# Hand-overs inside a four-stage kernel: products, rows, slots and weights put in another place

## The chip, the cores and the metric

One core of a Trainium2 chip. The metric is the device time of one execution in microseconds. Lower is better.

## The reference

Four stages, each with a layer norm, a shift and scale by condition rows, and a gated residual sum. The numbers are float32.

- stage 1 (`B, T, E = 4, 1024, 256`): a state-space layer with 512 inner channels and 16 states; its output `y * silu(z) @ W_out` is added to `x`
- stage 2: 8 experts, top 2 of each token
- stage 3: causal attention, 8 heads of 128, over 1024 tokens of each of the 4 batches
- stage 4: 16 experts with a capacity of 640 rows each, top 2 of each token, ranks counted in token order

```python
q = q + pe[None, None]
k = k + pe[None, None]
scores = jnp.where(causal, q @ k.T / sqrt(D), -inf)
out = (softmax(scores) @ v) @ Wo.T
...
ranks = cumsum(onehot)[sel] - 1
slot = jnp.where(ranks < capacity, flat_sel * capacity + ranks, sentinel)
padded = zeros.at[slot].set(x_rep)
h = gelu(einsum(padded, w1)); out_padded = einsum(h, w2)
```

## The kernel before

One program with one instruction stream for each engine; semaphores order them. The phases follow each other: state space (to about 976 us), routing and experts of layer 0 (to 1378), attention of layer 1 with the routing of layer 1 inside it (to 2585), experts of layer 1. Between phases all engines meet.

**State space, its end.** A chunk is 512 tokens, there are 8. For each of 64 steps (`STEPS`) ScalarE makes a decay in a PSUM bank (`da_ps`, a ring of four), VectorE scans it and multiplies by C (`output`, writing `hc`), and TensorE sums it into `y_ps` (`sum_states`). Then `y` is copied, turned back (`turn_back`), copied again, gated on POOL in two halves (`gate_y`, blocks 0 and 1, then 2 and 3), and `out_product` multiplies it by `w_out`, four blocks and one product with the identity that adds `x`, for each of the chunk's four 128-token tiles. For chunks 0 to 6 this lies inside the next chunk's steps; for the last one nothing runs beside it. `hc_at` and `w_ready` count what it waits for.

**Attention.** The unit is the query tile, 128 queries of one head: `N = 64` of them in a batch (`HEADS` 8 by `TPB` 8), tile `n` with `n % 8` giving how many of the key tiles it sees. The four batches are unrolled for the first and last, and a loop for the two between (`batches`). For tile `n` TensorE emits, in this order: `score(n)`; a piece of the projection of the next head (`project`, six pieces a head: two of q, two of k, two of v, at `n % 8` in `PROJECT`); `turn(n - 2)`, which transposes the normalised probabilities; `turn_rows` of the next batch's layer-norm rows at `TURN`; `weigh`, the product with the values, six tiles behind. VectorE masks and takes the maximum (`maximum(n)`), normalises tile `n - 1`, takes the projected pieces to SBUF (`take_piece`), keeps the outputs (`keep`). ScalarE does the exponentials and copies what TensorE has turned. Scores go through two PSUM tensors of two banks, `s_ps`; the pieces of head 0 (`bank`) and the output products of a batch's end go through the same ones, the pieces of heads 1 to 7 through `qk_ps`.

At a batch's end `output(t)` makes 8 products (16 instructions) for each of eight 128-token tiles; two of them (`EARLY_OUT`) come ahead of the last weighing. VectorE gates and adds each (`out_added`). The next batch's pieces of head 0 wait for all of these, and `score(0)` for all six pieces.

At the start of the phase VectorE adds two halves of the sum of layer 0 (`sums0`, `more0`), tile by tile, takes statistics of eight tiles, normalises eight rows, TensorE turns each through one bank, ScalarE copies it to `h_b`, and then all six pieces of head 0 are projected. The sync engine's queue loads, in this order: the four halves of `x` and `more`, the condition rows of three kinds for four batches (`load_mods`), the gate weights, the positions, `w_o`, then the next batch.

**Routing inside attention.** The routing of batch `b - 1` is laid out over the query tiles of batch `b`: rows at `R_NORM`, logits at `R_PAIR`, picks at `PICK`, the count of ranks on TensorE at `RANK = 52`, and on VectorE at `SLOTS` the weights (tile 52), the ranks (53) and the slots (54). POOL then sends, for each of the eight 128-token tiles of the batch, two indirect transfers (`scatter`, one for each choice) to `slots1`, both after the score of one query tile. The rows of batch `b + 1` are normalised on VectorE from tile `NORM = 53` on.

**Last experts.** 16 experts in turn; two sets of weights (`w1`, `w2`) and of rows (`xs`) are held. At the start of the phase the queue loads the gates' rows, then for experts 0 and 1 the routed rows and both weights.

## Time and profile before

| | us |
|---|---|
| median of three runs | 2908.6 |
| lowest, highest | 2907.63, 2910.3 |
| the profiled execution's own time | 2909.66 |
| its span, first to last instruction | 2907.9 |
| TensorE busy, of the span | 2492.8 (86%) |
| VectorE busy | 2103.6 (72%) |
| ScalarE busy | 1296.4 (45%) |
| POOL busy | 1234.4 (42%) |
| mean granted clock of TensorE, of full speed | 0.932 |

PE is TensorE's matmul part, PEld its weight loads, which overlap it, DVE is VectorE, ACT ScalarE, POOL GpSimd, SP the sync engine; SPq is its queue of transfers. A float32 product counts as two PE instructions, a transpose as one. An idle time in brackets stands before the instruction whose row it is in, with what ended it. A granted clock of 1.00 is 2.4 GHz, 0.50 is 1.2 GHz.

### The profile page before, as it was taken

The page shows a single profiled execution, that of the slowest core. Times are in us where ns is not written, and L with a number is a line of the kernel's source. Part 1 is how long each engine was busy: PE and PEld are TensorE (multiplying, and loading weights), DVE is VectorE, ACT ScalarE, POOL GpSimd, SP SyncE. Part 2 cuts the span into 40 slices and gives each one's busy share as a digit, 9 for nine tenths or more (in the row PEclk, how much of TensorE's full clock was granted, in tenths as well). Part 3 has the DMA queues.
Part 4 walks back from the last instruction along what each step waited for, and adds up shares of the span by engine and source line. Part 5 has one row for each costly group of instructions (what it writes and reads, how often), then busy time and mean ns, then how long its engine had stood idle before and what let it go on. Part 6 is the DMA issues. An engine that isn't in the chain of part 4 may idle for free. (4 is left out here: it accounts for less than half of the span.)

```text
span 2907.9 us, 39192 instructions
## 1 busy us (share of the span) xinstructions
PE 2492.8 (86%) x12341; PEld 1792.0 (62%) x12342; DVE 2103.6 (72%) x4277; ACT 1296.4 (45%) x2563; POOL 1234.4 (42%) x531
## 2 busy tenths in 40 slices
PE   6677867868766759998799999999999999959998
PEld 4355545645545559998466666666666666647776
DVE  4999999999999566665666567766776677655554
ACT  4677677677665235554243324332433243311111
POOL 2799999999999036666000000020002000223344
PEclk8889989889986879999899999999999999969999
DMA  4645555555556254334300010001001000035554
GB/s 147 192 154 186 178 174 186 176 171 192 165 180 206 81 173 64 64 63 61 114 1 1 1 48 1 1 31 34 1 1 34 15 1 1 30 112 128 129 130 74
DMA packets 150845, 268.98 MB, mean 92 GB/s; under 512 B 18316, under 2 KB 107324, under 8 KB 150172
## 3 DMA queue, kind: packets, MB, share of 16 engines
q1 hardware_dynamic: 121916, 227.12, 24.3%
q0 software_dynamic: 28224, 37.78, 7.7%
q10 hardware_dynamic: 544, 2.10, 0.2%
q8 instruction: 81, 1.33, 0.2%
q14 instruction: 80, 0.66, 0.1%
HBM read 209.52 MB, written 57.43 MB: 92 GB/s over the span
## 5 line engine op out<-in xcount | busy, mean ns | idle before, releaser
L765 POOL TENSOR_TENSOR dbx<-u,b_all 128x2048 f32<-128x2048 f32 x128 | 578.6, 4535 | 71.2 <-DVE u L844 33.3
L1805 POOL DMA_INDIRECT slots<-at_r_rows,slot_of x64 | 62.7, 980 | 1140.3 <-DVE slot_of L2220 1048.5
L649 ACT ACTIVATE da_ps<-delta,a_neg 128x512 f32<-128x512 f32 x512 | 347.9, 689 | 132.7 <-DVE hc L917 124.5
L2066 ACT COPY at_pt<-at_pt_ps 128x512 f32<-128x512 f32 (+3 forms) x384 | 171.7, 483 | 504.5 <-PE at_pt_ps L1935 501.1
L469 PE MATMUL y_ps<-ident,hc 128*128 128x128 f32 x1536 | 246.5, 305 | 87.6 <-DVE hc L917 87.0
L1924 PE MATMUL at_s_ps<-at_qk 128*128 128x512 f32 (+3 forms) x768 | 291.4, 489 | 3.1 <-DVE at_v L2269 3.1
L1948 PE MATMUL at_o_ps<-at_pt,at_v 128*128 128x512 f32 (+3 forms) x768 | 288.6, 487 | 0.3 <-issue 0.3
L469 PEld LDWEIGHTS y_ps<-ident,hc 128*128 128x128 f32 x1536 | 200.6, 158 | 143.0 <-DVE hc L917 115.4
L2055 ACT ACTIVATE at_probs<-at_s_ps,at_small 128x128 f32<-128x128 f32 (+7 forms) x256 | 192.2, 751 | 202.2 <-DVE at_small L2280 198.9
L917 DVE TENSOR_TENSOR hc<-da_ps,c_all 128x512 f32<-128x512 f32 x384 | 257.7, 673 | 0.0
L907 DVE TENSOR_TENSOR_SCAN da_ps<-da_ps,state,dbx 128x512 f32<-128x512 f32 x192 | 243.4, 1277 | 4.5 <-ACT da_ps L649 3.6
L907 DVE TENSOR_TENSOR_SCAN da_ps<-da_ps,dbx 128x512 f32<-128x512 f32 x192 | 231.9, 1217 | 12.8 <-ACT da_ps L649 8.0
L1924 PEld LDWEIGHTS at_s_ps<-at_qk 128*128 128x128 f32 x768 | 137.0, 190 | 127.0 <-issue 94.9
L1908 PE MATMUL at_qk_ps<-at_h_b,w_qkv 128*128 128x512 f32 x448 | 211.9, 595 | 1.5 <-DVE at_rank L2206 0.9
L2276 DVE TENSOR_TENSOR at_s_ps<-at_s_ps,at_later 128x128 f32<-128x128 f32 x256 | 75.9, 296 | 187.0 <-PE at_s_ps L1924 186.0
L1534 POOL DMA_INDIRECT out<-e_ys,e_row_i x80 | 125.3, 1566 | 193.2 <-DVE e_ys L1643 153.6
L2278 DVE TENSOR_REDUCE at_small<-at_s_ps 128x1 f32<-128x128 f32 (+7 forms) x256 | 194.0, 758 | 8.8
L1935 PEld LDWEIGHTS at_pt_ps<-ident,at_probs 128*128 128x128 f32 x1152 | 137.1, 141 | 73.0 <-issue 52.0
L1935 PE MATMUL at_pt_ps<-ident,at_probs 128*128 128x128 f32 x1152 | 169.5, 274 | 9.5 <-DVE at_probs L2288 9.1
L1591 ACT ACTIVATE e_hid<-e_h_ps 128x320 f32<-128x320 f32 x128 | 55.9, 437 | 249.0 <-PE e_h_ps L1557 248.5
L1948 PEld LDWEIGHTS at_o_ps<-at_pt,at_v 128*128 128x128 f32 x768 | 127.4, 191 | 60.6 <-issue 57.2
L774 POOL TENSOR_TENSOR own_h<-own_h,c_all 128x2048 f32<-128x2048 f32 x32 | 144.9, 4528 | 29.5 <-DVE own_h L907 29.5
(385 smaller groups left out, 5021.6 us busy)
## 6 DMA issues: line engine op xcount, KB each, us to landing
b_all<-bc_rows SPq DMA_DIRECT2D x128, 512.0 KB, 4.4
c_all<-bc_rows SPq DMA_DIRECT2D x128, 512.0 KB, 5.1
e_w<-L_ffn_w SPq DMA_DIRECT2D x32, 512.0 KB, 5.5
slots<-zeros SPq DMA_DIRECT2D x40, 260.0 KB, 6.1
e_xs<-slots SPq DMA_DIRECT2D x16, 650.0 KB, 7.1
w<-L_ffn_W SPq DMA_DIRECT2D x24, 384.0 KB, 8.6
more<-zeros SPq DMA_DIRECT2D x16, 256.0 KB, 5.4
sums<-x SPq DMA_DIRECT2D x8, 512.0 KB, 6.9
```

Source lines behind the costliest of these rows:

```text
L469: mm = nc.tensor.matmul(y_ps[par][:, at], source[:, at], sh.ident[:], start=False, stop=(last and j == CT - 1), is_transpose=True)
L649: nc.scalar.activation(da_ps[s % RING_DA][:], delta[:, c % 2, m, :], ACT.Exp, scale=sh.a_neg[:, m, n:n + 1]).then_inc(S["da_ready"], 1)
L765: nc.gpsimd.tensor_tensor(dbx[:, at % RING_DBX], pair, rows, ALU.mult).then_inc(S["dbx_ready"], 1)
L907: nc.vector.tensor_tensor_scan(out, h, dbx[:, at % RING_DBX, i // 2, par, :], 0.0 if c % CPB == 0 else state[:, s:s + 1], ALU.mult, ALU.ad ...
L917: nc.vector.tensor_tensor(hc[:, v % RING_H, :], da_ps[s % RING_DA][:], c_all[:, at % RING_C, s % GS // 2, :], ALU.mult).then_inc(S["hc_rea ...
L1908: last = nc.tensor.matmul(out, w_qkv[:, k, h, i // 2, :], h_b[:, i % 2, k, :], start=(k == 0), stop=(k == KE - 1))
L1924: last = nc.tensor.matmul(s_ps[n % 2][:, part * CH:end], qk[:, h % 2, 0, i * P:(i + 1) * P], qk[:, h % 2, 1, part * CH:end], start=True, s ...
L1935: last = nc.tensor.transpose(pt_ps[half][:, j % CT, :], probs[:, n % 3, j * P:(j + 1) * P], sh.ident[:])
L1948: last = nc.tensor.matmul(o_ps[:, first:], v[:, h % 2, j, :], pt[half][:, j, first:], start=(j == 0), stop=(j == (half + 1) * CT - 1))
L2055: nc.scalar.activation(probs[:, n % 3, 0:(i + 1) * P], s_ps[n % 2][:, 0:(i + 1) * P], ACT.Exp, bias=small[:, n % 4, 1:2], scale=SCALE, acc ...
L2066: nc.scalar.copy(pt[i // CT][:, half * CT:half * CT + m, at], pt_ps[half][:, 0:m, :]).then_inc(S[f"copied{half}"], 1)
L2278: nc.vector.reduce_max(small[:, n % 4, 0:1], s_ps[n % 2][:, 0:(i + 1) * P], AX_X).then_inc(S["max_taken"], 1)
```

## The change

It has six parts. (1) The output products of the last chunk of the state-space phase go to the banks `da_ps`, and the identity and blocks 0 and 1 of each tile are multiplied ahead of the last gate, two tiles of them between the last steps. (2) At the start of attention the first batch goes in two halves: its condition rows are loaded first, the first half is added in one instruction on VectorE, the second in one on POOL; three pieces of head 0 are projected from the first four rows; the pieces' order is 0, 2, 4, 1, 3, 5; other loads wait for the second half. (3) The pieces of head 0 of later batches wait for their own bank alone, and `score(0)` for five pieces. (4) At tiles 64 and 65 the first seven heads' part of two output tiles is multiplied, ahead of the turns. (5) The slots are made at two tiles, weights earlier, the next batch's rows two tiles later; in batches 1 and 2 a scatter is sent after each of sixteen query tiles, in the last batch two after each of eight. (6) `w1`, `w2` and the gates' rows of the last experts lie in the place of `w_qkv` and are loaded after its last use; the first routed rows are loaded alone.

```diff
+            def last_first_blocks(j):
+                pair, i = j // 2, j % 2
+                if i == 0:
+                    pe.wait_ge(S["hc_ready"], hc_at(LAST, STEPS - RING_DA + pair) + 1)
+                    pe.wait_ge(S["y_gated"], LAST * HALVES + 1)
+                    pe.wait_ge(S["w_ready"], B)
+                out = da_ps[pair][:, i * E:(i + 1) * E]
+                nc.tensor.matmul(out, sh.ident[:], sh.x[:, LAST * CT + j, :], start=(i == 0), stop=False, skip_group_check=True)
+                for k in range(2):
+                    nc.tensor.matmul(out, u[:, LAST % 2, k, j * P:(j + 1) * P], sh.w_out[:, k, :], start=False, stop=False, skip_group_check=True)
+
+            def last_blocks(pair):
+                if pair == 0:
+                    pe.wait_ge(S["y_gated"], CHUNKS * HALVES)
+                for i in range(2):
+                    j = pair * 2 + i
+                    for k in range(2, MD):
+                        mm = nc.tensor.matmul(da_ps[pair][:, i * E:(i + 1) * E], u[:, LAST % 2, k, j * P:(j + 1) * P], sh.w_out[:, k, :],
+                                              start=False, stop=(k == MD - 1), skip_group_check=True)
+                mm.then_inc(S["out_done"], 1)
...
                     sum_states(c, k)
+                    if c == LAST and k >= STEPS - 3 and k < STEPS - 1:
+                        last_first_blocks(k - STEPS + 3)
...
-                turn_back(CHUNKS - 1, m)
+                turn_back(LAST, m)
+            for j in range(2, CT):
+                last_first_blocks(j)
             for pair in range(2):
-                out_product(CHUNKS - 1, pair)
+                last_blocks(pair)
...
+                bank = da_ps[pair] if c == CHUNKS - 1 else proj_ps[pair]
...
-                if not early(e, 2):
-                    sp.wait_ge(y_done, (e - 1) * S1)
+                if early(e, 2):
+                    return
+                sp.wait_ge(y_done, (e - 1) * S1)
...
             load(0, 0, 0)
+            sp.wait_ge(x_in[0], 16)
             load(1, 1, 0)
...
-        SLOTS = (RANK, RANK + 1, RANK + 2)
-        NORM, TURN, COPY = N - 11, N - 8, N - 7
+        SLOTS = (RANK - 2, RANK + 1, RANK + 2, RANK + 3)
+        NORM, TURN, COPY = N - 9, N - 8, N - 7
...
+            sp.dma_start(sh.mods[:, 0:2, 0, :], d["mod_rows"][1, 0:2, 0].partition_broadcast(P)).then_inc(S["mods0_in"], 16)
             for th in range(CPB):
...
-            load_mods(sp, d, sh, 1, 0, S["mods_in"])
+            sp.wait_ge(x_first[1], 32)
+            sp.dma_start(pos[:], d["posT"]).then_inc(S["pos_in"], 16)
+            sp.dma_start(sh.mods[:, 0:2, 1:B, :], d["mod_rows"][1, 0:2, 1:B].partition_broadcast(P)).then_inc(S["mods_in"], 16)
+            sp.dma_start(sh.mods[:, 2], d["mod_rows"][1, 2].partition_broadcast(P)).then_inc(S["mods_in"], 16)
             sp.dma_start(gate_w[:], d["gate_wT"].rearrange("(k p) n -> p k n", p=P)).then_inc(S["gate_in"], 16)
-            sp.dma_start(pos[:], d["posT"]).then_inc(S["pos_in"], 16)
             sp.dma_start(w_o[:], d["woT"].rearrange("(h p) e -> p h e", p=P)).then_inc(S["w_o_in"], 16)
...
+            sp.wait_ge(S["qk_done"], B * HEADS * PIECES + 1)
+            sp.dma_start(sh.gates[:], d["mod_rows"][1, 5].partition_broadcast(P)).then_inc(sh.gates_in, 16)
+            for e in range(2):
+                sp.dma_start(sh.w1[:, e], d["L1_ffn_w1"][e].rearrange("(k p) f -> p k f", p=P)).then_inc(sh.w1_in[e], 16)
+                sp.dma_start(sh.w2[:, e], d["L1_ffn_w2"][e].rearrange("(m p) f -> p m f", p=P)).then_inc(sh.w2_in[e], 16)
             store_out(B - 1)
...
+            late = slice(CT, TPB)
+            pool.wait_ge(x_first[1], 32)
+            nc.gpsimd.tensor_tensor(sh.x[:, late], sh.x[:, late], more[:, late], ALU.add).then_inc(first_summed[1], 1)
...
-                    if count is None:
-                        pool.wait_ge(S["scored"], (rb + 1) * N + SLOTS[2] + 1 + j)
                     for k in range(2):
+                        if count is None:
+                            pool.wait_ge(S["scored"], (rb + 1) * N + SLOTS[3] + 1 + (2 * j + k if rb < B - 2 else j))
                         nc.gpsimd.indirect_dma_start(out=d["slots1"], out_offset=bass.IndirectOffsetOnAxis(ap=sh.slot_of[:, k, i:i + 1], axis=0),
                                                      in_=r_rows[:, j, :], in_offset=None).then_inc(S["scattered"], 16)
...
+        FIRST_PIECES = (0, 2, 4, 1, 3, 5)
+        first_turned = (qk_ps, o_ps)
...
+            return qk_ps[:] if h else bank(FIRST_PIECES.index(i))
...
-            pe.wait_ge(S["w_o_in"], 16)
...
+                    out = first_turned[j % 2]
+                    pe.wait_ge(S["h_copied"], max(j, 1))
...
+            for j in range(CT):
                 turn_rows(0, j)
...
-                    if h > 0:
+                    if h > 1 or i > 0:
                         pe.wait_ge(S["qk_ready"], b * (HEADS * PIECES) + h * PIECES + i + 1)
-                    elif i >= 4:
-                        pe.wait_ge(S["qk_ready"], b * (HEADS * PIECES) + i - 2)
+                    else:
+                        pe.wait_ge(S["qk_ready"], b * (HEADS * PIECES) + h * PIECES + i)
+                    products(h, i, out)
...
+                def project_first(place):
+                    if place >= 4:
+                        pe.wait_ge(S["qk_ready"], b * (HEADS * PIECES) + place - 2)
+                    elif not first_batch:
+                        pe.wait_ge(S["out_added"], b * TPB + place - 2)
+                    products(0, FIRST_PIECES[place], bank(place))
...
-                        pe.wait_ge(S["qk_ready"], b * (HEADS * PIECES) + h * PIECES + (4 if h else PIECES) + 1)
+                        pe.wait_ge(S["qk_ready"], b * (HEADS * PIECES) + h * PIECES + (4 if h else PIECES - 1) + 1)
+                    if n == CT:
+                        pe.wait_ge(S["qk_ready"], b * (HEADS * PIECES) + PIECES + 1)
...
+                    if HEADS - 1 in heads:
+                        last.then_inc(S["out_done"], 1)
+
+                if first_batch:
+                    pe.wait_ge(S["h_copied"], CT + 1)
+                    for place in range(PIECES // 2):
+                        project_first(place)
+                    for j in range(CT, TPB):
...
+                for place in range(PIECES // 2 if first_batch else 0, PIECES):
+                    project_first(place)
...
+                    if n >= N:
+                        if n == N:
+                            if first_batch:
+                                pe.wait_ge(S["w_o_in"], 16)
+                                pe.wait_ge(S["gate_in"], 16)
+                                pe.wait_ge(S["consts_ready"], 12)
+                            pe.wait_ge(S["exp_done"], b * N + N - 1)
+                        output(n - N, range(HEADS - 1))
...
-                        pe.wait_ge(S["exp_done"], b * N + N - 1)
                         pe.wait_ge(S["attn_ready"], b * (2 * HEADS) + 2 * HEADS)
-                    output(t)
+                    output(t, range(HEADS - 1, HEADS))
...
+            act.wait_ge(S["first_var"], 1)
+            nc.scalar.activation(sh.var[:, 0:CT], sh.var[:, 0:CT], ACT.Sqrt).then_inc(S["first_std"], 1)
+            for j in range(CT):
+                copy_rows(0, j)
+            act.wait_ge(S["var_ready"], 1)
+            nc.scalar.activation(sh.var[:, CT:TPB], sh.var[:, CT:TPB], ACT.Sqrt).then_inc(S["std_ready"], 1)
+            for j in range(CT, TPB):
                 copy_rows(0, j)
...
+            def slot_sums(rb, k):
+                v = nc.vector
+                for source, dst in ((cand, slot), (rank, valid)):
+                    linked(rb, v.tensor_tensor(scores[:], mask[:, k], source[:], ALU.mult))
+                    linked(rb, v.tensor_reduce(dst[:, k], scores[:], AX_X, ALU.add))
+
+            def slots_begun(rb):
+                dve.wait_ge(S["rank_taken"], rb + 1)
+                linked(rb, nc.vector.tensor_tensor(cand[:], rank[:], offs[:].rearrange("p (o e) -> p o e", o=1).broadcast_to([P, TPB, NE]), ALU.add))
+                slot_sums(rb, 0)
+
...
+                slot_sums(rb, 1)
...
+            early = slice(0, CT)
+            dve.wait_ge(x_first[0], 32)
+            nc.vector.tensor_tensor(sh.x[:, early], sh.x[:, early], more[:, early], ALU.add).then_inc(first_summed[0], 1)
+            first_link = link_on(dve, S["first_chain"])
+
+            def first_rows(th, var_ready, std_ready, rstd_ready):
+                dve.wait_ge(first_summed[th], 1)
+                at = slice(th * CT, (th + 1) * CT)
+                for j in range(th * CT, (th + 1) * CT):
+                    nc.vector.bn_stats(sh.stats[:, j, :], sh.x[:, j, :]).then_inc(S["stats_in"], 1)
...
+                dve.wait_ge(S[std_ready], 1)
+                nc.vector.reciprocal(sh.rstd[:, at], sh.var[:, at]).then_inc(S[rstd_ready], 1)
+                dve.wait_ge(S[rstd_ready], 1)
+                if th == 0:
+                    dve.wait_ge(S["mods0_in"], 16)
+                for j in range(th * CT, (th + 1) * CT):
+                    normalise_rows(0, j)
+
+            first_rows(0, "first_var", "first_std", "first_rstd")
+            first_rows(1, "var_ready", "std_ready", "rstd_ready")
+            dve.sem_inc(S["summed"], TPB)
+            dve.sem_inc(S["stats_chain"], STATS_OPS)
...
-                for i in range(PIECES):
+                for i in FIRST_PIECES:
                     take_piece(0, i)
+                if first_batch:
+                    dve.wait_ge(S["mods_in"], 32)
...
+                            (weights, take_ranks, slots_begun, slots)[SLOTS.index(n)](b - 1)
...
+        place = sh.w_qkv[:].rearrange("p k h c f -> p (k h c f)")
+        sh.w1 = place[:, 0:2 * KE * F1].rearrange("p (r k f) -> p r k f", r=2, k=KE)
+        sh.w2 = place[:, 2 * KE * F1:2 * KE * F1 + 2 * MF1 * E].rearrange("p (r m e) -> p r m e", r=2, m=MF1)
+        sh.gates = place[:, 2 * KE * F1 + 2 * MF1 * E:2 * KE * F1 + 2 * MF1 * E + B * E].rearrange("p (b e) -> p b e", b=B)
```

What is left out declares semaphores, passes the place of a piece or the turned bank along, or reads the gates' rows from `gates` and not from `sh.mods[:, 2]`.

## Rows read from the trace of the kernel before

**Rows 1.** Busy time by stretches: PE, PEld, DVE, ACT, POOL busy, granted clock, DMA share, GB/s.

```profile
1500.00:1600.00 100.00, 100.00 (x444) 62.83 (x443) 67.30 (x174) 42.15 (x102) 0.00 (x0) 1.00 0.00 1
...
2500.00:2600.00 100.00, 62.09 (x273) 47.36 (x272) 55.19 (x182) 18.89 (x32) 19.43 (x22) 0.78 0.25 82
```

**Rows 2.** Waits of TensorE from 1418 to 2514: who for whom, us in total, times, longest.

```profile
PE at_pt_ps L1935 <- DVE at_probs L2288: 9.1, 9, 1.7
...
PE at_qk_ps L1913 <- DVE at_v L2269: 6.6, 5, 2.6
```

**Rows 3.** Order of time, end of the state-space phase: start us, us, what, [idle before <-releaser].

```profile
957.51 1.25 PE L469 MATMUL y_ps<-ident,hc 128*128 128x128 f32 x8 [0.97 <-DVE hc L917]
...
960.85 2.34 POOL L796 TENSOR_TENSOR u<-u,gate 128x1024 f32<-128x1024 f32 x1 [13.07 <-ACT u L581]
...
963.24 3.78 PE L479 MATMUL proj_ps<-w_out,u 128*128 128x256 f32 x8 [3.09 <-POOL u L796]
...
970.38 1.89 PE L479 MATMUL proj_ps<-w_out,u 128*128 128x256 f32 x8
...
974.27 0.59 PE L481 MATMUL proj_ps<-x,ident 128*128 128x256 f32 x2
```

**Rows 4.** Busy time of two short stretches there; columns as in rows 1.

```profile
955.00:960.00 5.00, 3.85 (x29) 2.97 (x28) 3.05 (x6) 1.57 (x3) 0.00 (x0) 0.99 0.00 0
...
963.00:967.00 4.00, 3.76 (x9) 3.02 (x10) 0.00 (x0) 0.00 (x0) 0.19 (x1) 0.50 0.00 0
```

**Rows 5.** Order of time, start of attention.

```profile
1384.36 0.42 DVE L2121 TENSOR_TENSOR x<-x,at_attn 128x256 f32<-128x256 f32 x1 [11.77 <-DMA at_attn<-more]
...
1392.22 0.21 ACT L2025 ACTIVATE var<-var 128x8 f32<-128x8 f32 x1 [12.59 <-DVE var L2144]
...
1392.78 0.48 DVE L2242 SCALAR_TENSOR_TENSOR at_rows<-x,mean,mods 128x256 f32<-128x256 f32 x1
...
1405.46 8.93 PE L1908 MATMUL at_s_ps<-at_h_b,w_qkv 128*128 128x512 f32 x16 [0.46 <-ACT at_h_b L2041]
...
1409.37 0.69 DVE L2265 TENSOR_TENSOR at_qk<-at_s_ps,at_pos 128x512 f32<-128x512 f32 x1 [8.19 <-PE at_s_ps L1908]
...
1418.74 0.92 PE L1924 MATMUL at_s_ps<-at_qk 128*128 128x128 f32 x4 [0.78 <-DVE at_v L2269]
```

**Rows 6.** Order of time, from batch 0 to batch 1.

```profile
1682.31 7.13 PE L1908 MATMUL at_s_ps<-at_h_b,w_qkv 128*128 128x512 f32 x16 [0.52 <-DVE at_gated L2418]
...
1693.80 0.92 PE L1924 MATMUL at_s_ps<-at_qk 128*128 128x128 f32 x4 [0.78 <-DVE at_v L2269]
```

**Rows 7.** Order of time, last tiles of batch 0.

```profile
1644.71 0.99 PE L1935 MATMUL at_pt_ps<-ident,at_probs 128*128 128x128 f32 x7 [1.11 <-DVE at_probs L2288]
...
1648.34 7.15 PE L1956 MATMUL at_s_ps<-at_w_o,at_attn 128*128 128x256 f32 x32 [0.88 <-DVE at_attn L2292]
```

**Rows 8.** Order of time, slots in batches 1 and 3; last, all scatters by their line.

```profile
1898.71 0.28 DVE L2211 TENSOR_TENSOR at_cand<-at_rank,at_offs 128x128 f32<-128x128 f32 x1
...
1906.59 3.03 PE L1913 MATMUL at_qk_ps<-w_qkv,at_h_b 128*128 128x128 f32 x16 [2.61 <-DVE at_v L2269]
...
2484.66 2.05 PE L1913 MATMUL at_qk_ps<-w_qkv,at_h_b 128*128 128x128 f32 x16 [0.96 <-issue]
...
L1805 POOL DMA_INDIRECT slots<-at_r_rows,slot_of x64: 954/960/1285, 1902.9 to 2582.8; - x64
```

**Rows 9.** Order of time, start of the last experts.

```profile
2585.97 0.43 SPq L1507 DMA_DIRECT2D e_xs<-slots  x1
...
2589.91 1.10 DVE L1650 TENSOR_TENSOR mods<-mods 128x256 f32<-128x256 f32 x3 [17.02 <-DMA mods<-mod_rows]
...
2592.46 1.11 PE L1546 MATMUL e_x_ps<-ident,e_xs 128*128 128x128 f32 x4 [23.94 <-DMA e_xs<-slots]
```

**Rows 10.** Busy time of the stretch after it; columns as in rows 1.

```profile
2593.00:2597.00 4.00, 3.24 (x11) 1.76 (x10) 3.23 (x13) 0.00 (x0) 0.00 (x0) 0.50 1.07 374
```

**Rows 11.** Order of time, VectorE at tile 61 of batch 0.

```profile
1635.96 0.30 DVE L2276 TENSOR_TENSOR at_s_ps<-at_s_ps,at_later 128x128 f32<-128x128 f32 x1 [1.40 <-PE at_s_ps L1924]
```

88 lines of the change are left out of this document (42 added, 46 removed).

## The prediction

> **What bounds the kernel now.** I read the busy time by stretches first. In the attention of the second layer TensorE is busy 99 to 100% of a stretch at the full clock, while VectorE is at two thirds; in the 100 us that hold the hand-over to the last experts TensorE has 62% [rows 1]. So the steady part is bound by TensorE, whose work the change leaves as it is, and only the places where TensorE stands still can pay. Next the waits of TensorE inside attention: 9.1 us for the normalised probabilities and 6.6 us for a head's value pieces are the long ones [rows 2]. Then the order of time at each place that the diff touches: the end of the state-space phase, where the last output products begin only after POOL's gate [rows 3]; the start of attention, 40 us from the hand-over to the first score [rows 5]; the three hand-overs between batches [rows 6]; the end of a head's last tiles, four times [rows 7]; the slots of the routed rows, three times [rows 8]; the start of the last experts [rows 9]. The chain that ended last, on the page, lies in the experts alone and is of no help for what comes before.
>
> **1. End of the state-space phase.** Before: the gate on POOL ends at 963.19, then 20 products of 256 columns run as 40 instructions to 974.86 [rows 3]; the first 20 at the half clock, since TensorE had stood still before [rows 4]. At the full clock 8 instructions take 1.89 us, a pace of 0.216; 8 at the half clock take 3.78. After: only the products of the last two blocks wait for the gate, 16 instructions, 3.5 us at the full clock. The other 24 move ahead. Two groups of 6 (1.3 us each) go between the last sums: the first fits where TensorE waits for `hc` from 956.4, the second pushes the last sum, and with it copies, turn and gate, back by 1.2 us, to 964.4. The other 12 instructions (2.6 us) fill the wait for the gate, so I expect the clock to stay up. End 967.9 for 974.9: 7.0 us saved. Bounds: the last 16 at the half clock, 6.9 us, leave 3; 7.5 if the second group pushes nothing.
>
> **2. Start of attention.** Before: first sum at 1384.36, variances ready at 1392.2, rows from 1392.78, first projection 1405.46, first score 1418.74 [rows 5]. The eight tiles' sums and statistics take 6.4 us of the first 7.9, 0.8 a tile, and seven small operations the rest. After: the first layer-norm rows come down the queue ahead of the sums, a quarter of a megabyte; I put 0.7 us on it (bounds 0 and 1.5; 0.25 MB at 374 GB/s [rows 10] is that): 1385.1. Four tiles, their add in one instruction, 2.6; small operations 1.4; root and reciprocal 0.6, with the added wait on the reciprocal 0.75; four rows at 0.92, 3.7; turn and copy of the last 1.1: 1394.65. Three pieces: the first 3.9 at the half clock as before, then 1.7 and 1.9: 1402.1. Meanwhile VectorE has rows 4 to 7 ready by 1400.8; their turns go through two banks in 2.2 us, paced by ScalarE's copies of 0.37. Three pieces more, 5.3: first score 1409.5. Saved 9.2 us. POOL's add of the other four tiles has the size of its gate, 2.34 us [rows 3], and is covered: VectorE works on the first half until 1393.5. The transfers of positions and the other rows now wait for the second half and have 9 us until they are needed; uncovered, each of these in turn costs what it is late. Bounds 5 and 11.
> The Trainium skill, SBUF — State Buffer, section "Who interferes with whom", states that a VectorE operation with two SBUF inputs and a GpSimd one that reads SBUF exclude each other for a whole instruction. By that rule POOL's add holds the small chain of the first half for up to 1.2 us, and this term is 8.0 in place of 9.2. No row of this trace puts such a pair side by side; the sum goes without it, inside the bounds.
>
> **3. Between batches, three times.** TensorE waits 0.52 us for the gate of the last output tile and 0.78 for the second half of the values [rows 6]. The first goes, since piece 0 needs only the bank of tile 4; the second moves to the fifth query tile, long after. 1.3 us each, 3.9; the first batch's 0.78 is in term 2. Low 2, if the tiles that follow give it back to VectorE.
>
> **4. End of a batch, four times.** Before turning tile 62 TensorE stands 1.1 us for VectorE; then 0.88 us for head 7's first half, then 32 instructions of output for two tiles, 7.15 us [rows 7]. After: 28 of them, 6.0 us, run in front of the turns of tiles 62 and 63. They cover the 1.1; the 0.88 stays, because the turns and the last weighing are now late by as much and the copy follows them. 1.15 us each, 4.6. Bounds 1 (if queueing ahead of the turns delays ScalarE's copies into the last weighing) and 6.
>
> **5. Slots and scatters.** In batches 1 and 2 VectorE runs thirteen slot operations in a row from 1898.71 on, 3.9 us, plus a row of the next batch; the value piece is taken late and TensorE stands 2.6 us; the 16 instructions behind it take 3.03 us for the usual 1.95. In batch 3 the same wait is 0.96 [rows 8]. After: five operations (1.6 us) at tile 54 and eight (2.3 us) at tile 55, with weights three tiles earlier and the rows starting at 55 for 53. The wait at the piece goes; but tile 55 now has 2.3 + 0.96 + its own 3.9 us on VectorE, and I follow that to tile 58: TensorE is 1.2 us earlier there by the maxima, 1.7 with two small gaps closed. 1.7 × 2 + 1.1 for batch 3 + 0.3 for batch 0 (rows alone) = 4.8; I take 4.3, because two rows land on tiles 61 and 62. Bounds 0 and 7. The rows there cost nothing while VectorE has the room: it stands 1.40 us before the maximum of tile 61, and a row is two operations of 0.48 [rows 5, 11]. The scatters themselves cost POOL 0.96 us each, 64 as before [rows 8]; they are waited for only by the routed rows of the next batch, 29 tiles in, and spreading 16 of them over 16 tiles ends at its 8th tile. I put nothing on that edit: it frees nothing that TensorE waits for.
>
> **6. Start of the last experts.** Before: gates' rows, then the routed rows at 2585.97, landed at 2592.4 while four weight transfers were behind it; TensorE turns them from 2592.46 [rows 9]. After: that transfer is first and alone, so 0.4 us of issue goes and half a megabyte in front of it. The half megabyte of gates' rows, first in the queue, landed 4.3 us after its issue [rows 9]; at the 374 GB/s of the next stretch [rows 10] it takes 1.4 of that, so 2.9 are start. 650 KB take 1.8, and so they land at 2585.6 + 2.9 + 1.8 = 2590.3: 2.1 us saved. I take 2.0. The 2.5 MB of gates and weights move to 2487, after the last projection, and have 95 us. Bounds 0.4 and 3.
>
> **Sum.** 7.0 + 9.2 + 3.9 + 4.6 + 4.3 + 2.0 = 31.0 us. The terms add, as the phases follow each other and attention is bound by TensorE between them. The profiled execution took 2909.7 us (span 2907.9), 1.1 us above the median of the runs: 2908.6 - 31.0 = 2877.6. The low ends give 3 + 5 + 2 + 1 + 0 + 0.4 = 11.4, the high ones 38.
>
> **Rivals.**
> A. The starts do not pay: the transfers land late and the clock is low. The first sums come 1.5 us later, the turns between the two groups of pieces cost another 2, the last 16 products run at the half clock, and the routed rows land where they did. Terms 1, 2 and 6 give 3 + 6 + 0.4. For it: both starts are cold, 0.50 in a stretch after a wait [rows 4]. Against: nothing stands still for long in the new order. 31.0 less 4.0 + 3.2 + 1.6 is 22.2: 2886.4.
> B. The small gaps move: in a stretch at 99% TensorE what is given back comes as another wait on VectorE, so terms 3, 4 and 5 give 2 + 1 + 0. For it: VectorE is the releaser of nearly all of TensorE's waits [rows 2]. 31.0 less 1.9 + 3.6 + 4.3 is 21.2: 2887.4. A and B together: 2896.2.
> C. Slower: the rows of the next batch, moved to tiles 55 to 62, make VectorE the bound of each of these eight tiles in three batches, 24 tiles. It loses from 1.3 us a tile on (31.0 / 24). For it: VectorE's room beside a row is 1.40 less 0.96 us [rows 11]. Against: a whole row is 0.96 us, and only tiles 61 and 62 get one more than before; if every tile lost 1.5 us, 36 us: 2913.6.
>
> **How the numbers follow.** Forecast 0.62, A 0.15, B 0.17, A and B together 0.03, C 0.02, and 0.01 that what is moved hides nothing at all. The forecast's own range is 2871 to 2883. The one for 8 in 10 reaches to A and B and down to most of the high ends: 2870 to 2889. No change means within 0.2%, 5.8 us, about what a measurement of this kernel tells from nothing. Faster 0.96, same 0.02, slower 0.02.
>
> **What would show it.** Products after the last gate: 16 in 3.5 us. First score some 31 us after the hand-over to attention, not 40. No wait of TensorE for the gated rows at a batch's head. 28 output products ahead of the turn of tile 62, and no idle there. At tile 55 no wait over 1 us. Routed rows landed within 4.5 us of their issue. It is wrong if the first pieces start after 1397, if the page shows new waits on the probabilities of tiles 61 to 63 above 1 us, or if the steady pace of a head changes at all.

## The result, and the profile after

| | median us | runs | ratio to before, 95% |
|---|---|---|---|
| before | 2909.2 | 2907.6 to 2910.3 (4) | |
| after | 2877.75 | 2877.3 to 2882.7 (4) | 0.9896 [0.9879, 0.9913] |
| after, measured again | 2878.8 | 2877.9 to 2879.6 (4) | 0.9901 [0.9886, 0.9916] |

The forecast was 2877.6. The total came out; its parts did not all have the size that was put on them, and the errors cancelled. To see that, the lengths of the phases are more use than the time: they are differences between starts in one profile. Over the profiles whose edit does not touch a phase, the batches repeat best: batches 0 and 2 to 0.1 us, batch 1 to 0.4 (285.98 to 286.34), batch 3 to 0.1 but for a stop of 1.1 to 1.6 us in some (last section). The others are looser: from the last `hc` to the last output product 0.6 us, to the hand-over 2.3, from the hand-over to the first score 0.7, the experts behind their first row 1.6. The start of the last `hc` in the state-space phase alone moved by 4 us over all profiles (954.9 to 959.0). By "the last `hc`" is meant the row that holds the last two. The profiled executions took 2909.7, 2882.7 and 2879.6 us, their spans 2907.9, 2881.0 and 2877.9.

| phase, us | before | after | again |
|---|---|---|---|
| start of the last `hc` | 956.78 | 959.00 | 956.96 |
| from there to the end of the last output product | 18.08 | 12.08 | 12.09 |
| from there to the hand-over to attention | 421.57 | 416.12 | 415.95 |
| hand-over to first score | 40.39 | 34.58 | 34.36 |
| batch 0, from first score to first score | 275.06 | 271.92 | 271.91 |
| batch 1 | 290.69 | 286.10 | 286.08 |
| batch 2 | 291.12 | 285.46 | 285.46 |
| batch 3, to its last output product | 274.90 | 272.43 | 271.30 |
| last output product to the last experts' stage | 35.10 | 35.50 | 35.33 |
| from there to the first turned row | 6.85 | 4.15 | 4.17 |

By stretches, one batch of the profile before and of the one after (columns as in [rows 1]). The 4.6 us less are 2.3 of idle time and 2.3 of busy time of TensorE. The granted clock is 0.99 before and 1.00 after, and the 16 instructions behind the wait of 2.61 us in [rows 8] took 3.03 us for the usual 1.95; that all of the 2.3 is of this kind is not shown:

```profile
1693.80:1984.49 290.69, 280.34 (x1252) 182.69 (x1252) 198.05 (x513) 98.89 (x244) 15.98 (x16) 0.99 0.06 19
```
```profile
1681.62:1967.72 286.10, 278.09 (x1255) 181.03 (x1253) 197.64 (x513) 99.30 (x244) 9.20 (x9) 1.00 0.06 18
```

The end of the state-space phase after, TensorE, ScalarE and POOL (answers to [rows 3]). L493 and L495 are the groups moved ahead of the gate, L503 the 16 instructions behind it:

```profile
958.06 1.33 PE L469 MATMUL y_ps<-ident,hc 128*128 128x128 f32 x8
959.23 0.60 PE L493 MATMUL da_ps<-x,ident 128*128 128x256 f32 x2
959.66 1.03 PE L495 MATMUL da_ps<-w_out,u 128*128 128x256 f32 x4
960.53 0.60 PE L469 MATMUL y_ps<-ident,hc 128*128 128x128 f32 x4
960.96 0.60 PE L493 MATMUL da_ps<-x,ident 128*128 128x256 f32 x2
961.40 1.03 PE L495 MATMUL da_ps<-w_out,u 128*128 128x256 f32 x4
962.26 0.60 PE L469 MATMUL y_ps<-ident,hc 128*128 128x128 f32 x4
964.96 2.35 POOL L824 TENSOR_TENSOR u<-u,gate 128x1024 f32<-128x1024 f32 x1 [14.95 <-ACT u L608]
967.36 3.72 PE L503 MATMUL da_ps<-w_out,u 128*128 128x256 f32 x16 [0.51 <-POOL u L824]
```

Its clock by windows (answers to [rows 4]), 1.00 of full speed in both, where it was 0.50 behind the gate before; the second is the one behind the gate:

```profile
961.00:966.00 5.00, 4.67 (x29) 4.06 (x28) 0.00 (x0) 2.25 (x4) 1.04 (x1) 1.00 0.00 0
967.00:971.00 4.00, 3.64 (x16) 2.96 (x16) 0.75 (x2) 0.59 (x1) 0.31 (x1) 1.00 0.00 0
```

The start of attention after (answers to [rows 5]); the hand-over is at 1375.1. The sixth line is the one to look at: an operation on 128x4, 0.17 us everywhere else, takes 2.24 beside POOL's add:

```profile
1375.12 0.37 SPq L1766 DMA_DIRECT2D mods<-mod_rows  x1
1383.46 1.23 DVE L2332 TENSOR_TENSOR x<-x,at_attn 128x1024 f32<-128x1024 f32 x1 [14.29 <-DMA at_attn<-more]
1384.72 1.41 DVE L2339 BATCH_NORM_STATS2 stats<-x 128x6 f32<-128x256 f32 x4
1386.16 0.17 DVE L2343 TENSOR_TENSOR mean<-stats 128x4 f32<-128x4 f32 x1
1386.24 2.34 POOL L1840 TENSOR_TENSOR x<-x,at_attn 128x1024 f32<-128x1024 f32 x1 [8.80 <-DMA at_attn<-more]
1386.36 2.24 DVE L2344 TENSOR_SCALAR mean<-mean 128x4 f32<-128x4 f32 x1
1395.05 5.63 PE L1967 MATMUL at_s_ps<-at_h_b,w_qkv 128*128 128x512 f32 x8 [0.46 <-ACT at_h_b L2116]
1409.70 0.82 PE L1985 MATMUL at_s_ps<-at_qk 128*128 128x128 f32 x4
```

TensorE at the head of batch 1 and at the end of batch 0 after (answers to [rows 6] and [rows 7]). No wait is left at the head before the first score; at the end, 14 + 14 output products stand ahead of the turns, no wait of 1.11 is left there, and 0.78 of the 0.88 stays:

```profile
1634.62 3.19 PE L2017 MATMUL at_s_ps<-at_w_o,at_attn 128*128 128x256 f32 x14
1637.65 0.93 PE L1996 MATMUL at_pt_ps<-ident,at_probs 128*128 128x128 f32 x7
1638.84 3.19 PE L2017 MATMUL at_s_ps<-at_w_o,at_attn 128*128 128x256 f32 x14
1641.87 1.04 PE L1996 MATMUL at_pt_ps<-ident,at_probs 128*128 128x128 f32 x8
1643.91 1.13 PE L2017 MATMUL at_s_ps<-at_w_o,at_attn 128*128 128x256 f32 x4 [0.78 <-DVE at_attn L2400]
1671.19 3.60 PE L1967 MATMUL at_s_ps<-at_h_b,w_qkv 128*128 128x512 f32 x8
1681.62 0.82 PE L1985 MATMUL at_s_ps<-at_qk 128*128 128x128 f32 x4
```

The slots in batch 1 after (answers to [rows 8]): no 2.6 at the value piece, but waits for probabilities of 1.45 and 1.12 in its place:

```profile
1896.70 0.98 PE L1996 MATMUL at_pt_ps<-ident,at_probs 128*128 128x128 f32 x7 [1.45 <-DVE at_probs L2396]
1899.88 1.09 PE L1996 MATMUL at_pt_ps<-ident,at_probs 128*128 128x128 f32 x8 [1.12 <-DVE at_probs L2396]
```

The first row of the last experts after (answers to [rows 9]), 4.2 us behind its issue:

```profile
2561.09 4.52 SPq L1532 DMA_DIRECT2D e_xs<-slots  x2
2565.26 1.12 PE L1573 MATMUL e_x_ps<-ident,e_xs 128*128 128x128 f32 x4 [21.71 <-DMA e_xs<-slots]
```

### The profile page after: what moved, and what is told of

It reads as the page before. It is cut to its first block, busy times and chain, and to the rows that moved or that the text cites. A ratio compares the mean times of both kernels' runs of the same rounds, so it can differ in the third digit from the quotient of the medians.

```text
span 2881.0 us, 39211 instructions
## 1 busy us (share of the span) xinstructions
PE 2484.7 (86%) x12341; PEld 1786.8 (62%) x12342; DVE 2103.1 (73%) x4278; ACT 1297.7 (45%) x2564; POOL 1238.3 (43%) x532
## 4 chain that ended last, share of the span: by engine, by line
PE 44%; DVE 4%; issue 2%; ACT 1%; DMA 1%; POOL 0%; another core or an unknown queue 0%; DVEq 0%; SPq 0%; ACTq 0%; POOLq 0%
PE at_o_ps L2009 8%; PE at_s_ps L1985 7%; PE at_qk_ps L1967 6%; PE e_h_ps L1584 5%; PE e_y_ps L1595 5%; PE at_s_ps L2017 4%; PE at_pt_ps L1996 4%; PE at_qk_ps L1972 3%; PE at_s_ps L1967 1%; DVE at_small L2386 1%; PE e_x_ps L1573 1%; PE at_s_ps L1972 0%; PE at_qk_ps L1905 0%; DVE at_s_ps L2384 0%; DVE at_v L2377 0%
## 5 line engine op out<-in xcount | busy, mean ns | idle before, releaser
L1595 PE MATMUL e_y_ps<-w_qkv,e_hid 128*128 128x256 f32 x640 | 152.3, 382 | 5.6 <-ACT e_hid L1618 5.6
```

The source lines that it names most:

```text
L1595: last = nc.tensor.matmul(y_ps[(r + t) % 2][:], hid[:, m, t * P:(t + 1) * P], w2[:, r, m, :], start=(m == 0), stop=(m == MF1 - 1))
```

## The experiments

Each kernel is the changed one with one edit. "Lost" and "won" are against the column "again" above. In the runs beside them before took 2907.0 us (first four), 2909.1 (next four) and 2907.1 (last four), and with the state-space phase wandering as it does, medians tell 2 us apart at best; below that the verdict rests on the lengths of phases.

**The changed kernel again.**

> The changed kernel once more, unaltered. Its profiled execution took 2882.7 us, the three others 2877.3 to 2878.1; inside the profiled one the state-space phase ran 2.2 us behind the trace of before by its last sums, in code that the change does not touch. Theory: the state-space phase, which waits on transfers all the time, varies by a few us from one execution to the next. Then the median stays at 2877.8, this profile may fall anywhere from 2877 to 2883, and what is behind is again inside the state-space phase, with another size; the first score, counted from the hand-over to attention, comes at 34.6 us as before. Rival: the profile itself costs this kernel 5 us. Then the profiled execution is again at 2882 to 2883 and the others at 2877 to 2878.

Measured: 2877.9 to 2879.6, the profiled execution 2879.6. The rival falls. Of the 3.1 us between the two profiles, 2.0 are in the state-space phase ahead of the last `hc`, and 1.1 in batch 3, where in the first profile VectorE, ScalarE and POOL stand still at once (last section).

**End of the state-space phase as before.**

```
-                    if c == LAST and k >= STEPS - 3 and k < STEPS - 1:
-                        last_first_blocks(k - STEPS + 3)
...
-            for j in range(2, CT):
-                last_first_blocks(j)
             for pair in range(2):
-                last_blocks(pair)
+                out_product(LAST, pair)
```

> The changed kernel with the end of the state-space phase as before: all 40 output instructions of the last chunk behind POOL's last gate. Sum theory: the end is worth its term of 7.0 us, and nothing later gives any of it back: 2877.8 + 7.0 = 2884.8, and from the end of the gate to the last product 11.7 us instead of 3.8. Rival (the trace of after at its face value): the hand-over to attention was only 3.2 us earlier than before, so the part is worth 3.2: 2881.0. The profile tells them apart by the time from the start of the last `hc` to the hand-over, which does not depend on how the phase went before that.

Measured: 2883.6 us, 4.8 lost. From the last `hc` to the last product 18.06 us for 12.09, to the hand-over 421.6 for 416.0: 6.0 and 5.7 lost. Both prices were wrong, 7.0 and 3.2; the 3.2 of the first profile had 2.2 of the phase's own wandering in it. Its rows: the gate begins 4.09 us after the last `hc` at 954.88, where in the two profiles of the changed kernel it is 5.96:

```profile
954.88 1.28 DVE L941 TENSOR_TENSOR hc<-da_ps,c_all 128x512 f32<-128x512 f32 x2
955.62 1.25 PE L469 MATMUL y_ps<-ident,hc 128*128 128x128 f32 x8 [1.01 <-DVE hc L941]
958.97 2.34 POOL L820 TENSOR_TENSOR u<-u,gate 128x1024 f32<-128x1024 f32 x1 [13.08 <-ACT u L604]
961.36 3.78 PE L479 MATMUL proj_ps<-w_out,u 128*128 128x256 f32 x8 [3.09 <-POOL u L820]
```

The 12.09 is not the only length of the changed end. No other edit touches it, and yet in seven of the twelve profiles that have it the gate begins 5.33 to 5.35 us after the last `hc` and the last product ends at 11.45 to 11.47; in four (the two of the changed kernel among them) it is 5.94 to 5.97 and 12.06 to 12.09, and in one 5.73 and 11.85. In the seven, as in the profile before, the granted clock rises from 0.50 to 1.00 some 1.6 us ahead of the last `hc`; in the four only 0.3 to 0.4 us ahead of it. So undoing is worth 6.0 to 6.6 us. Why the clock rises later in some is open. Two rows of the shorter form, from the last run below:

```profile
957.66 1.27 DVE L945 TENSOR_TENSOR hc<-da_ps,c_all 128x512 f32<-128x512 f32 x2
963.00 2.34 POOL L824 TENSOR_TENSOR u<-u,gate 128x1024 f32<-128x1024 f32 x1 [14.34 <-ACT u L608]
```

**Output products behind the last turns.**

```
-                        output(n - N, range(HEADS - 1))
...
-                    output(t, range(HEADS - 1, HEADS))
+                    output(t)
```

> The changed kernel with the output products of tiles 0 and 1 behind the last turns and the last weighing again, as one piece. Sum theory: each of the four ends of a batch loses 1.15 us, 4.6 in all: 2882.4; the wait of 1.1 us ahead of the turn of tile 62 is back four times and a wait of 0.8 to 0.9 for head 7's first half stays. Rival (the gaps move): TensorE finds the lost time back at the head of the next batch, where VectorE then has more of its work behind it; a loss of 1: 2878.8.

Measured: 2884.5 us, 5.7 lost; the four batches are 273.41, 287.40, 286.95 and 273.16 us, so 1.50, 1.32, 1.49 and 1.86 lost, 6.2 together. Nothing is given back at the next head: the rival falls. TensorE in batch 0 of it:

```profile
1633.54 0.98 PE L1996 MATMUL at_pt_ps<-ident,at_probs 128*128 128x128 f32 x7 [0.98 <-DVE at_probs L2393]
1637.17 3.04 PE L2017 MATMUL at_s_ps<-at_w_o,at_attn 128*128 128x256 f32 x13 [0.88 <-DVE at_attn L2397]
```

**Head of a batch as before.**

```
-                    elif not first_batch:
-                        pe.wait_ge(S["out_added"], b * TPB + place - 2)
-                    products(0, FIRST_PIECES[place], bank(place))
+                    elif place == 0 and not first_batch:
+                        pe.wait_ge(S["out_added"], b * TPB + 1)
+                    products(0, FIRST_PIECES[place] if first_batch else place, bank(place))
```

> The changed kernel with the head of batches 1 to 3 as before: the first head's pieces in the order 0 to 5, and all of them behind the last gated tile of the batch before. The first batch keeps its two halves. Sum theory: 0.52 us for the gate and 0.78 for the second half of the values come back at three heads, 3.9 in all: 2881.7. Rival (the gaps move): the first tiles of the next batch have waited for VectorE anyway, and only the half comes back, 2.0: 2879.8.

Measured: 2880.4 us, 1.6 lost; batches 272.72, 286.22, 286.46: 0.81, 0.14 and 1.00, 1.95 together. The wait for the gated rows is back (0.52, 0.52, 0.61), the one of 0.78 for the values is not: my expectation overlooked that the first score of the changed kernel waits for one piece less, and this edit leaves it so. The 0.78 before each first score is therefore shown gone by the profiles, not by an experiment. In batch 1 only 0.14 is lost: a new wait of 0.17 at that head in the changed kernel goes with the edit. A size of 0.14 there is not told from nothing, since batch 1 took 285.98 to 286.34 in the two profiles of the changed kernel and three whose edit is elsewhere. One row of it:

```profile
1668.43 7.13 PE L1967 MATMUL at_s_ps<-at_h_b,w_qkv 128*128 128x512 f32 x16 [0.52 <-DVE at_gated L2528]
```

**Two scatters a tile.**

```
-                            pool.wait_ge(S["scored"], (rb + 1) * N + SLOTS[3] + 1 + (2 * j + k if rb < B - 2 else j))
+                            pool.wait_ge(S["scored"], (rb + 1) * N + SLOTS[3] + 1 + j)
```

> The changed kernel with one edit undone: POOL sends both scatters of a query tile behind that tile's scores, 16 over eight tiles, in batches 1 and 2 (here for the routed rows of batches 0 and 1), not one a tile over sixteen. Sum theory (the prediction put nothing on this edit): 2878.8 as the changed kernel ran beside it, batches 1 and 2 at 286.1 and 285.5 us each within 0.2. Rival: two scatters of 0.97 us in a row disturb VectorE's and ScalarE's work at the tiles 56 to 63, where TensorE already waits 1.45 and 1.12 us for probabilities; at 0.1 to 0.2 us a tile that is 1.6 to 3.2 us in two batches: 2880.4 to 2882.

Measured: 2880.3 us, ratio 0.9900 against 0.9901: no change. Batches 1 and 2 are 286.43 and 285.59, 0.35 and 0.13 longer. The wait at tile 54's turn is 1.51 for 1.45. The first is hardly more than what batch 1 does by itself (up to 286.34), so one scatter a tile for two is worth half a microsecond at most, and perhaps nothing.

**Slots and rows as before, and rows alone.** `all_slots` is `slots_begun` and `slots` in a row; the second kernel has the last pair of lines only.

```
-        SLOTS = (RANK - 2, RANK + 1, RANK + 2, RANK + 3)
+        SLOTS = (RANK, RANK + 1, RANK + 2, RANK + 3)
-                            (weights, take_ranks, slots_begun, slots)[SLOTS.index(n)](b - 1)
+                            (weights, take_ranks, all_slots, lambda rb: None)[SLOTS.index(n)](b - 1)
-        NORM, TURN, COPY = N - 9, N - 8, N - 7
+        NORM, TURN, COPY = N - 11, N - 8, N - 7
```

> The changed kernel with the slots in one piece of thirteen operations, the weights at tile 52 and the rows of the next batch from tile 53, all as before; the scatters stay where the change has put them. The recorded term says 4.3: 2883.1. From the lengths of the batches, what is left for this part once the end of a batch (1.3 to 1.85 each) and the head (0.8, 0.1, 1.0, and 0.78 each for the weaker wait of the first score) are taken off is 2.4, 2.4 and 1.7 in batches 1 to 3, 6.5 together: 2885.3. Batch 0, where only the rows move, stays at 271.9. Rival (the gaps move): 1 or less, 2879.8.

> The changed kernel with the rows of the next batch alone moved back, from tile 55 to tile 53; slots and weights stay as the change has them. If the rows are what loaded VectorE around the slots, batches 1 and 2 lose 1 to 1.5 us each and batch 3, which makes no rows, nothing: 2881.3. If it is the splitting of the slots alone, nothing: 2878.8. Two rows earlier take 1.9 us of VectorE ahead of the slots instead of behind them.

Measured: both, 2881.9 us, batches 1 and 2 at 287.66 and 286.47 (1.58 and 1.01 lost), batch 3 at 273.89 (2.6 longer: 1.0 from the slots, the rest such a stop as in the last section); rows alone, 2880.7 us, 287.30 and 286.56 (1.22 and 1.10 lost), batch 3 at 272.62, of which 1.1 to 1.3 is such a stop as in the last section and not theirs. So the rows make most of it in the two middle batches. With both undone the wait of 2.5 at the value piece is back, and in batch 1 the two for probabilities are gone (in batch 2 the one of 1.12 stays); with the rows alone they are 2.14 and 1.12. In batch 3, too, a wait of 0.95 at the value piece is back, released by VectorE's `at_v`. The row of batch 1 with both undone:

```profile
1889.84 3.47 PE L1972 MATMUL at_qk_ps<-w_qkv,at_h_b 128*128 128x128 f32 x16 [2.51 <-DVE at_v L2381]
```

**Slots, rows and scatters as before.** The three edits together, the scatters from `SLOTS[3] + j`.

> The changed kernel with slots, rows and scatters all three as before the change: two scatters a tile over eight tiles, from tile 55. Slots and rows alone undone gave batches 1 and 2 of 287.66 and 286.47 us, the spread of the scatters alone 286.43 and 285.59, against 286.1 and 285.5 of the changed kernel. If the scatters are worth nothing (as recorded), batches 1 and 2 come at 287.7 and 286.5 again. Rival: with the thirteen slot operations in one piece, scatters in pairs disturb the tiles where VectorE is already behind, and part of the 0.8 and 1.4 us that the parts undone one by one leave unexplained in batches 1 and 2 is theirs: 288.4 and 287.5.

Measured: 2882.0 us; 287.58 and 286.44, batch 3 at 272.28: 1.50, 0.98 and 0.98 lost, 3.5 together, in batch 0 nothing. The scatters add nothing to it, and the rival falls.

**Rows two tiles later still.** ScalarE's loop runs one step longer for it.

```
-        NORM, TURN, COPY = N - 9, N - 8, N - 7
+        NORM, TURN, COPY = N - 7, N - 6, N - 5
```

> The changed kernel with the rows of the next batch, their turns and copies two tiles later still (rows from tile 57, turns from 58). In the changed kernel TensorE waits 1.45 and 1.12 us for probabilities at tiles 54 and 55's turns in batches 1 and 2, with VectorE busy without a gap on slots and rows. If those rows are what holds it, 1.9 us of VectorE's work leave this place and 1.5 to 2.3 us a batch are won, in batches 1 and 2: 2875.2. Rival: the last two rows now fall behind the last tiles, where the copies and gated outputs of the batch's end need VectorE, and lose there what is won, in batch 0 as well: 2878.8, or 1 us a batch slower: 2881.8.

Measured: 2875.5 us; batches 1 and 2 at 284.49 and 283.75, 1.6 and 1.7 won, batch 0 at 271.87 as it was. The waits at the same two turns:

```profile
1892.16 0.98 PE L1996 MATMUL at_pt_ps<-ident,at_probs 128*128 128x128 f32 x7 [0.30 <-DVE at_probs L2396]
1894.34 1.09 PE L1996 MATMUL at_pt_ps<-ident,at_probs 128*128 128x128 f32 x8 [0.33 <-DVE at_probs L2396]
```

**VectorE adds the second half.**

```
-            pool.wait_ge(x_first[1], 32)
-            nc.gpsimd.tensor_tensor(sh.x[:, late], sh.x[:, late], more[:, late], ALU.add).then_inc(first_summed[1], 1)
...
             first_rows(0, "first_var", "first_std", "first_rstd")
+            dve.wait_ge(x_first[1], 32)
+            nc.vector.tensor_tensor(sh.x[:, late], sh.x[:, late], more[:, late], ALU.add).then_inc(first_summed[1], 1)
```

> The changed kernel with one instruction moved to another engine: the second four tiles of the first batch are summed by VectorE, behind the rows of the first four, and not by POOL. In both traces of the changed kernel a VectorE operation on 128x4 (the mean, 0.17 us elsewhere) takes 2.24 and 2.33 us while POOL's add of 2.34 us runs. Theory: the two hold each other off, and the start of attention loses 2.1 us by it. Then that operation takes 0.17 again, and from the hand-over to the first score it is 34.4 - 2.1 = 32.3 us; VectorE's add of 1.23 us stands where rows 4 to 7 have 1.5 us of room and costs nothing. Rival: the long operation is an accident of something else (the end of a transfer), or the room is not there: 34.4 or more. The time of the whole is 2 us less: 0.9894 of before for 0.9901.

Measured: 2873.7 us, ratio 0.9889; hand-over to first score 31.56, 2.8 won (2.3 to 3.0 against all ten profiles that leave the start as changed). Of the 2.8, 2.2 lie between the first sum and the first piece, which is the held operation; the other 0.6 lie behind it, where the first 8 instructions took 5.40 us for 6.02. The median fell by 5.2, which the lengths do not bear out. The operation is back at its length:

```profile
1380.49 0.17 DVE L2340 TENSOR_TENSOR mean<-stats 128x4 f32<-128x4 f32 x1
1380.69 0.17 DVE L2341 TENSOR_SCALAR mean<-mean 128x4 f32<-128x4 f32 x1
```

**First rows behind the first half of the sums.** Line 1766 moves behind the transfers of the first half.

> The changed kernel with the first layer-norm rows (256 KB) issued behind the first half of the sums, not ahead of them. Theory: they cost what they take of the transfers in front of the first sum. The first sum began 6.0 us after the hand-over before the change and 8.3 and 7.65 after it; with them behind, it begins at 6.0 to 6.4 and the first score comes 1.3 to 2.3 us sooner, at 32.1 to 33.1 us from the hand-over. The rows are needed some 4 us after the first sum and are there by then. Rival: the recorded price, 0.7 us: 33.7. Or they now land too late for the first normalised row, and nothing is won: 34.4.

Measured: 2876.2 us, ratio 0.9896; first sum 5.8 us after the hand-over for 7.65, first score at 31.27, 3.1 won. POOL's add now begins behind the small operations, and what it holds off is the first normalised row, 2.23 us for 0.48:

```profile
1382.38 2.34 POOL L1841 TENSOR_TENSOR x<-x,at_attn 128x1024 f32<-128x1024 f32 x1 [7.63 <-DMA at_attn<-more]
1382.78 2.23 DVE L2325 SCALAR_TENSOR_TENSOR at_rows<-x,mean,mods 128x256 f32<-128x256 f32 x1
```

**The best of them.** The last three edits, and `if n == VAR + 1:` ahead of `variance(b - 1, "2")`.

> Four edits on the changed kernel together: VectorE adds the second half; the first layer-norm rows go behind the first half of the sums; the rows of the next batch two tiles later (3.3 us in the lengths of batches 1 and 2, measured alone); and the variance of the routed rows one tile behind that of the next batch's rows, since TensorE waits 1.70 us for probabilities there in each middle batch. If they add: 2.1 + 1.6 + 3.3 + 2 x 1.3 = 9.6 us less than the changed kernel, 0.9868 of before for 0.9901; first score 30.7 us from the hand-over, batches 1 and 2 at 283.2 and 282.4. Rival: the two edits at the start overlap (the first half is ready sooner, the second is late instead), and the wait at the variances moves one tile on: 5.5 us less, 0.9882.

Measured: 2869.6 us (2868.7 to 2872.2), ratio 0.9872 [0.9857, 0.9887], 8.4 us less than the changed kernel by the ratios to before, 9.2 by the medians, 7.5 by the lengths of the phases that the edits touch. First score at 30.67; batches 1 and 2 at 284.27 and 283.47. The two edits at the start give 3.7 together and not 2.8 + 3.1, they overlap: with the sums early, POOL's add falls on another operation and held that off for 1.75 only. The split of the variances is worth 0.2 to 0.3 a batch and not 1.3: the wait of 1.70 comes back as 1.51 one tile on, at a query or key piece, as its rival said:

```profile
1764.75 1.98 PE L1965 MATMUL at_qk_ps<-at_h_b,w_qkv 128*128 128x512 f32 x4 [1.51 <-DVE at_qk L2374]
```

## Why the prediction was right

| term | recorded | measured, with "again" | by | over all profiles that have it |
|---|---|---|---|---|
| 1 end of state space | 7.0 | 6.0 | undone | 6.0 to 6.6 |
| 2 start of attention | 9.2 | 6.0 | profiles | 5.8 to 6.5 |
| 3 between batches | 3.9 | 4.3 | 1.95 undone, 3 x 0.78 seen gone | |
| 4 end of a batch | 4.6 | 6.2 | undone | |
| 5 slots, rows | 4.3 | 3.5 | undone | |
| 6 last experts | 2.0 | 1.8 | profiles | 1.4 to 2.8 |
| sum | 31.0 | 27.8 | | |

Terms 2 and 6 were never undone by a run: their sizes are differences between profiles, with one profile of before. That the total still came within 1 us of its mark is luck: terms 1 and 2 gave less than recorded, term 4 more, and 3.0 us that the batches gained stand in no measured part.

The spans of the profile before and of the one taken again differ by 30.0, 2.2 more than the sum of the parts. The batches hold 3.0 more than the parts in them (17.0 for 14.0), and 0.8 is lost elsewhere. Of the 3.0, 0.7 in batch 2 is an idle time of TensorE in the profile before that nothing in the kernel releases; the other 2.3, in batches 1 to 3, stay open. The wait of 0.96 in batch 3, put down to "issue" in [rows 8], is not among them: it comes back at the same place with the slots undone, so it is of term 5.

**Term 1** was right in its mechanism: 16 instructions behind the gate, 3.72 us for the 3.5 recorded, at the full clock. The delay of the gate, put at 1.2 us, is 1.3 in seven profiles (5.33 to 5.35 us after the last `hc` for 4.07) and 1.9 in four, those in which the clock rises late; so by the profile it was right, or 0.7 too small. One reading of it was wrong and no term rests on it: not the first 20 of the 40 instructions before ran at the half clock, for at the recorded pace of 0.216 that makes 13.0 us for all, where 11.6 were measured.

**Term 2** is where the prediction was most wrong, by 3.2 us, and it went by two mis-sized parts. The first rows ahead of the sums were put at 0.7 us, their size at the rate of a full stretch; they cost 1.6 (7.65 for 6.0) in one profile, 2.3 in the other, and 1.4 to 2.3 over the ten that have them. The rates show where it goes (40 equal slices, 1372 to 1392 in the profile taken again, then 1377.5 to 1397.5 in the one before). With the rows first, four slices move 111 to 176 GB/s, and the seventh is the first with more than 370; with the sums first, only two are below 200 and the third moves 344. With the rows behind the first half of the sums, as in the run above, the third moves 346 and a dip to 162 comes later. So it is these rows that are slow, and not whatever stands first in the queue:

```profile
GB/s 8 0 0 14 176 131 111 135 223 334 371 375 385 387 360 354 338 354 336 234 92 25 0 0 66 205 188 401 342 363 387 338 389 393 295 194 160 198 307 371
```
```profile
GB/s 0 0 0 8 158 98 344 389 377 375 387 360 358 336 352 354 592 348 455 418 442 393 393 371 216 394 414 350 371 352 352 348 348 348 346 354 344 346 352 344
```

And "POOL's add is covered" was false: it cost 2.1 us, through a 128x4 operation. From the first sum to the first piece the recorded working makes 9.55 us; with POOL's add gone it is 9.51, with it 11.6 to 11.7. With both taken away the first score comes at 30.7 us; the forecast was 31.2.
The Trainium skill, SBUF — State Buffer, section "Who interferes with whom", was named in the prediction for a pair with two SBUF inputs, with 1.2 us as its price. The same section of the Trainium skill says that a `tensor_scalar` can also take the ports that VectorE shares with GpSimd, and that whoever issues first has them for the whole instruction. Both traces agree: POOL's add starts first, by 0.04 to 0.12 us, and VectorE's operation ends with it. The price read from the rule was too low: what is held is the rest of POOL's instruction, whatever the length of VectorE's.

That price stood in the trace of the kernel before, and the prediction's "no row of this trace puts such a pair side by side" was not so. At the start of the state-space phase a VectorE sum with two inputs in SBUF, 1.23 us by itself, takes 3.32, as it has to wait out the 2.2 us that are left of a POOL instruction:

```profile
51.85 4.51 POOL L765 TENSOR_TENSOR dbx<-u,b_all 128x2048 f32<-128x2048 f32 x1 [33.33 <-DVE u L844]
54.13 3.32 DVE L842 TENSOR_TENSOR delta<-delta,u 128x1024 f32<-128x1024 f32 x1 [2.36 <-ACT u L625]
```

**Term 3** held, with 0.78 counted as a whole at each head; behind the first score of a batch a wait of 0.14 became one of 0.33 to 0.37, so 0.2 of it is given back. **Term 4** was too small: its 1.15 was the wait ahead of tile 62 alone; undone it costs 1.3 to 1.9, of which 0.9 to 1.3 is that wait, and in batches 0 and 3 another 0.1 the longer one behind it; the rest no single row shows. **Term 5** held in the total, but not in "no wait over 1 us at tile 55": 2.6 at the value piece became 1.45 and 1.12 at the two turns behind it. So the stall moved there, and won 1.0 to 1.5 a batch net; that is a piece of rival B, which falls at the other two places. The zero put on the scatters was right (0.35 and 0.13 us). **Term 6**: counted from the start of the stage the row came 2.7 us sooner, not 2.1. In the profile taken again 0.9 of it went: from that row to the end of the span it is 316.4 us for 315.5. The clock was lower in the first 20 us of the experts, 0.76 of full speed for 0.80 (0.04 x 20 = 0.8 us), while the busy times in the two stretches behind are equal. It is not what a sooner row always costs: in the first profile of the changed kernel the clock was 0.80 there and 0.2 went, and over all the profiles with the change it was 0.75 to 0.83 and the rest took 315.0 to 316.6. Before and again:

```profile
2592.46:2612.46 20.00, 18.93 (x68) 13.40 (x69) 10.75 (x33) 3.50 (x8) 1.68 (x2) 0.80 0.43 146
```
```profile
2561.52:2581.52 20.00, 18.93 (x65) 13.09 (x65) 9.96 (x32) 3.50 (x8) 1.13 (x1) 0.76 0.24 67
```

Rival A came in half (the sums late, but the clock up and the rows early), C not at all: batch 0, which has the rows and no slots, is as long to 0.15 us with them at tile 53, 55 or 57.

## What to carry to other kernels

Cut a kernel's time into phases by starts that every profile has, and judge small edits by those lengths; but first see over several profiles what each length does by itself, here 0.1 us in one batch and 2 us at the end of the first stage. Work handed to GpSimd is not off VectorE's path if the two overlap; ask what VectorE runs in those microseconds, however small, and look in the whole trace for a pair that already meets. And when a stall goes, look where the busy engine's queue is longest next: here moving eight rows by two tiles more was worth 3.3 us, about as much as all of part 5.

## What the runs showed of the hardware

A VectorE operation of 0.17 us took 2.24 and 2.33 beside a POOL add of 2.34, and another of 0.48 took 2.23; with the add on VectorE none did.

Some executions have a stop of about 1 us in which VectorE, ScalarE and POOL all stand and start again together, with a transfer as releaser that has no part in it. It was in batch 3 of the first profile (at 2476.8), at other tiles in four of the runs above (two scatters a tile, slots and rows as before, rows alone, rows two tiles later), and not in the one taken again. What it is stays open:

```profile
2476.81 0.30 DVE L2384 TENSOR_TENSOR at_s_ps<-at_s_ps,at_later 128x128 f32<-128x128 f32 x1 [3.20 <-DMA x<-L_attn_x]
2476.86 0.48 ACT L2146 COPY at_pt<-at_pt_ps 128x384 f32<-128x384 f32 x1 [2.96 <-remote]
2477.05 0.97 POOL L1849 DMA_INDIRECT slots<-at_r_rows,slot_of  x1 [1.70 <-DMA x<-L_attn_x]
```
